# Moving a 128x512 add from VectorE to GpSimd in a message-passing graph kernel

## What is computed

```
h   = relu(layernorm(x))                       # no gain or bias
xn  = layernorm(h) * g1 + b1
msg = relu(xn[src] + edge_attr)
agg = segment_sum(msg, dst)                    # dst is sorted
t   = (1 + eps) * xn + agg
h2  = h + relu(t @ Wg1 + bg1) @ Wg2 + bg2
f   = gelu((layernorm(h2) * g2 + b2) @ Wf1 + bf1) @ Wf2 + bf2
out = x + h2 + f
```

## Time and profile before

| what | value |
|---|---|
| time, median of 3 runs | 1072.53 us (1070.97 to 1072.89) |
| the profiled execution: its own time, its span | 1073.02 us, 1071.3 us |
| TensorE busy | 992.9 us, 93% |
| VectorE busy | 978.7 us, 91% |
| ScalarE busy | 844.3 us, 79% |
| GpSimd busy | 799.9 us, 75% |
| L743, the add that is moved | 33.3 us in 49 instructions |

### The profile page before, as it was taken

How to read it: one execution, slowest core, us unless ns; L and a number is a source line. 1 busy time by engine, 2 the same in 40 slices (tenths; PEclk the granted TensorE clock), 3 DMA queues, 4 the chain that set the end, 5 groups by cost and what they waited for, 6 DMA issues and landing times. The chain is left out here.

```text
span 1071.3 us, 23085 instructions
## 1 busy us (share of the span) xinstructions
PE 992.9 (93%) x6684; PEld 850.1 (79%) x6684; DVE 978.7 (91%) x3499; ACT 844.3 (79%) x2158; POOL 799.9 (75%) x510
## 2 busy tenths in 40 slices
PE   1336999999999999999999999999999999999998
PEld 1225888888888888888888888888888888878887
DVE  5577999999999999999999999999999999988752
ACT  1247888888888888888888888888888888878773
POOL 6488787787787787887887877888878878866610
PEclk9858999999999999999999999999999999999999
DMA  7566676788887655555555554555565654443311
GB/s 234 139 189 161 161 191 185 177 245 233 234 242 216 134 135 130 135 135 127 138 136 123 138 142 118 139 142 117 142 140 114 143 141 112 120 102 92 58 57 40
DMA packets 110469, 156.87 MB, mean 146 GB/s; under 512 B 24836, under 2 KB 50608, under 8 KB 110335
## 3 DMA queue, kind: packets, MB, share of 16 engines
q1 hardware_dynamic: 70358, 128.99, 37.6%
q0 software_dynamic: 37760, 25.66, 19.3%
q10 hardware_dynamic: 2216, 0.66, 0.3%
HBM read 90.61 MB, written 64.61 MB: 145 GB/s over the span
## 5 line engine op out<-in xcount | busy, mean ns | idle before, releaser
L520 ACT ACTIVATE n_act<-p_f,bf1e_col 128x512 f32<-128x512 f32 x392 | 255.9, 679 | 149.4 <-PE p_f L875 141.5
L447 POOL DMA_INDIRECT aggr_sums<-e_merged,e_index x196 | 322.8, 1647 | 65.8 <-issue 49.8
L917 PE MATMUL p_out<-wf,n_act 128*128 128x128 f32 x3136 | 370.6, 276 | 0.0
L917 PEld LDWEIGHTS p_out<-wf,n_act 128*128 128x128 f32 x3136 | 357.6, 191 | 4.0
L456 POOL TENSOR_TENSOR n_rstd<-n_var,minus_half 128x12 f32<-128x12 f32 (+2 forms) x102 | 256.4, 2514 | 116.4 <-DVE n_var L827 59.6
L436 POOL DMA_INDIRECT e_x<-in_x,e_cols x196 | 214.6, 1095 | 61.6 <-issue 58.9
L875 PE MATMUL p_f<-n_z2T_high,wf_low 128*128 128x512 f32 x392 | 207.0, 528 | 11.9 <-issue 7.0
L875 PE MATMUL p_f<-n_z2T_high,wf_high 128*128 128x512 f32 x392 | 154.6, 395 | 0.0
L875 PE MATMUL p_f<-n_z2T_low,wf_high 128*128 128x512 f32 x392 | 153.9, 393 | 0.0
L672 DVE BATCH_NORM_STATS2 n_stat<-n_x 128x6 f32<-128x256 f32 x392 | 139.6, 415 | 0.1
L532 ACT ACTIVATE p_gout<-n_relu,n_rstd 128x128 f32<-128x128 f32 x392 | 129.3, 367 | 5.4 <-DVE n_x L799 5.2
(11 more groups left out here) (85 smaller groups left out, 1433.5 us busy)
## 6 DMA issues: line engine op xcount, KB each, us to landing
n_x<-in_x SPq DMA_DIRECT2D x97, 256.0 KB
n_aggr<-aggr_sums SPq DMA_DIRECT2D x97, 256.0 KB
out_dram<-n_out SPq DMA_DIRECT2D x97, 256.0 KB
aggr_sums<-zeros SPq DMA_DIRECT2D x26, 512.0 KB, 3.2
e_dst<-in_dst_rows SPq DMA_DIRECT2D x49, 256.0 KB
e_attr<-in_attr SPq DMA_DIRECT2D x48, 256.0 KB
aggr_sums<-zeros SPq DMA_DIRECT2D x12, 1024.0 KB
e_x<-in_x,e_cols POOLq DMA_INDIRECT x196
```

What stands on the lines that cost most here:

```text
L447: nc.gpsimd.indirect_dma_start(out=aggr, out_offset=bass.IndirectOffsetOnAxis(ap=e_index[0:r, s, j:j + 1], axis=0), in_=e_merged[0:r, s, j ...
L520: nc.scalar.activation(n_act[:, k, :, 0:b.rows], p_f[k % 2][:, :, 0:b.rows], ACT.Gelu, bias=bf1e_col[:, k:k + 1]).then_inc(s_act, 1)
L917: last = nc.tensor.matmul(p_out[0:b.rows, j, :], n_act[:, k, j, 0:b.rows], wf2[:, k, :], start=False, stop=(k == KF - 1), skip_group_check ...
```

## The change

`add_b1` leaves VectorE. The same instruction, on the same operands and with the same waits, stands in GpSimd's even step behind the first two gathers of a chunk. Its signal `s_eattrb` and the readers of it stay as they are.

```diff
@@ gpsimd, step @@
                 if 0 in halves and (c := edge(0)) is not None:
                     gather(c, range(0, PAIR))
+                if 0 in halves and (c := edge(2)) is not None:
+                    r, s = c.rows, c.slot(3)
+                    if c.is_number(0):
+                        pool.wait_ge(s_rows_out, 1)
+                    pool.wait_ge(q_attr[s], 16 * (c.uses(3) + 1))
+                    reached(pool, s_esum, c.at - 2)
+                    nc.gpsimd.tensor_tensor(e_attrb[0:r, s], e_attr[0:r, s], all_columns(b1_row, r),
+                                            ALU.add).then_inc(s_eattrb, 1)
                 if 1 in halves and 0 in halves:
                     merged_first(edge, apart)
@@ vector @@
-            def add_b1(c):
-
-                if c is not None:
-                    r, s = c.rows, c.slot(3)
-                    if c.is_number(0):
-                        dve.wait_ge(s_rows_out, 1)
-                    dve.wait_ge(q_attr[s], 16 * (c.uses(3) + 1))
-                    reached(dve, s_esum, c.at - 2)
-                    nc.vector.tensor_tensor(e_attrb[0:r, s], e_attr[0:r, s], all_columns(b1_row, r),
-                                            ALU.add).then_inc(s_eattrb, 1)
-
@@ vector, step @@
                 if 0 in halves or not halves:
                     first_half(edge(1), node)
-                    if 0 in halves:
-                        add_b1(edge(2))
```

## The result

| | median of runs | range |
|---|---|---|
| before | 1072.71 us (4 runs) | 1070.97 to 1073.06 |
| after | 1129.88 us (4 runs) | 1129.08 to 1132.31 |

The ratio is 1.0539, 95% interval 1.0522 to 1.0556: the change costs 57 us, 45 us beyond the upper end of the range. The profiled execution took 1129.86 us with a span of 1128.0, which is 56.7 above the span of before.

What follows compares the result with a forecast made beforehand. TensorE and VectorE looked full, VectorE's fullness costing 0.23 us a pair over TensorE's 19.80. 1073.0 - 5.7 (steady) + 1.6 (start) + 1.0 (end) = 1069.9, forecast as 1069.5 us; range 1063 to 1085.

Steps and rivals of the forecast that it cites:

- VectorE's need becomes 20.03 - 0.61 = 19.42 a pair: Steady stretch: without its add, VectorE needs 0.61 us less in each pair, 19.42, below TensorE's 19.80.
- TensorE's 19.80: Steady stretch: TensorE's own pace, 19.80 us a pair, when nobody waits for VectorE.
- VectorE is held up by the add's reads: Rival: VectorE's two-input L840 and L845 stand some 0.9 us while GpSimd's add streams; 1088 us, chance 0.14.
- the add's length: The 128x512 add on GpSimd: 1.25 us, the middle between 0.87 and 1.64.
- the 1.1 worked out beside it: The add on GpSimd by the Trainium skill's 2.6 cycles of 1.2 GHz an element: 1.1 us for 512 elements.
- 19.89: Steady stretch: GpSimd's need in a pair with the add, 20.03 - 1.54 + 1.40, taken as the new pitch.
- gathers land in time: Steady stretch: after the change 2.4 us remain from the last gather's end to VectorE's read; a landing takes 2.42.
- a bound on GpSimd: Rival: two inputs cost twice one, the add takes 1.64 + 0.15, GpSimd becomes the bound; 1086 us, chance 0.13.
- late gathers: Rival: landings take 3.2 us, not 2.42, so VectorE waits 0.8 us in each pair; 1083 us, chance 0.06.
- 1.6 at the start: Before 109 us: adds ahead of later gathers delay VectorE; 1.6 us lost, taken between 0 and 3.2.
- 1.0 at the end: Last chunk: an add stands ahead of its second two gathers; 1.0 us lost, taken between 0 and 1.4.

Runs made afterwards that it cites:

- 1: Changed kernel with GpSimd's add moved ahead of the two gathers, directly behind the second scatter; 1148.9 us, 1.0699 of the kernel before.
- 3: Changed kernel with VectorE's n_out ahead of n_var; 1122.89 us, 1.0438 of the kernel before.
- 6: Changed kernel with the whole add directly behind the odd step's 128x12 `pow`, four e_attr buffers and earlier loads; 1085.96 us, 1.0111 of the kernel before.
- 8: Changed kernel with the whole add behind the odd step's second scatter, one chunk earlier; 1138.26 us, 1.0607 of the kernel before.
- 12: Whole add behind the odd step's `pow`, n_var moved ahead of n_in on VectorE; 1112.12 us, 1.036 of the kernel before.
- 15: Changed kernel with a `pow` of 128x1 between the gathers and the add; 1126.03 us, 1.0498 of the kernel before.
- 5: No add of b1 on any engine, e_attr loaded in the even step into six buffers; 1062.66 us, 0.9892 of the kernel before.
- 13: Whole add behind the odd step's `pow`, n_var between the third and fourth n_in; 1068.38 us, 0.9961 of the kernel before.
- 2: Kernel before, VectorE keeping its add, plus a 128x6 `pow` on GpSimd in the add's place; 1078.47 us, 1.0043 of the kernel before.
- 10: Kernel before, VectorE keeping its add, plus a 128x1408 memset on GpSimd behind the first gathers; 1097.64 us, 1.0227 of the kernel before.
- 16: Whole add behind the odd step's `pow`, n_var between third and fourth n_in, first five chunks added by VectorE; 1064.09 us, 0.9928 of the kernel before.

## Why the prediction was wrong

**The step that failed** is "VectorE's need becomes 20.03 - 0.61 = 19.42 a pair", taken with nothing added. The 19.42 itself holds within 0.25: a single pair less its hold leaves 19.2 to 19.5 (1, 3, 6, 8, 12, 15 and the changed kernel). TensorE's 19.80 holds too (19.82 in 5). But 1.66 us of hold came on top, and by 1, 3, 6, 8, 12 and 13 this depends on what stands beside the add: the same instruction on the same engine costs between 0.1 and 2.3 us a pair, and the pitch follows 19.42 plus the hold, while a longer `pow` in the same place costs no hold (2).

**The rival had the mechanism and not the size.** "VectorE is held up by the add's reads" was given 0.14, a stall of 0.9 and 1088 us. Two things were wrong. The first is the place: it let the add run for 0.4 us before L840 came, since only instructions with two SBUF inputs were counted. Between stands n_var, 128x4, which can be held as well, and which VectorE reaches right behind n_in. The second is the time: the hold began 0.4 us ahead of the add's record, at the end of n_in (502.43 against 502.84), and a gather alone does that to a `tensor_scalar`, as the trace of the kernel before shows (last section). With 1.66 the rival's own formula gives 20.03 - 0.61 + 1.66 = 21.08, and 41 x 1.05 = 43 us for the stretch, where 44.3 were measured.

**What misled the chance** was the row against it, a `pow` that ran beside four L845 without holding them. That was read rightly, and 2 shows it again, but a `pow` of 6 to 16 columns is no model for a stream of 512. The Trainium skill, "SBUF — State Buffer", section "Who interferes with whom", was cited for two SBUF inputs only. The same section also names `tensor_scalar` among the instructions that can contend without a second input, where its operands allow a mode that takes both ports, and says that a GpSimd instruction which only writes leaves two-input instructions alone. The runs agree with both: n_var stood beside the memset and four e_zg did not (10); that n_var is in such a mode no run shows. The section says further that one SBUF input outside such a mode doesn't contend, and the statistics agree (13). By the section a GpSimd instruction that starts first keeps the ports for its whole length, and there the runs differ: a `pow` holds nothing for its length of 1.48 (2).

**What was right:** the add's length (1.25 forecast, the middle of two bounds, taken for want of a reason, so the hit is partly luck; 1.31 measured, 1.26 behind a `pow`, and the 1.1 worked out beside it is too low); that GpSimd isn't the bound (it has 1.5 us a pair to wait in the changed kernel, and with the add in its list it keeps a pitch of 19.81 in 13, so its need is no more than that and not 19.89); that gathers land in time (two short waits in the even stretch of 5, four in that of the changed kernel, 2.1 us together). The rivals of a bound on GpSimd and of late gathers fall.

**The ends.** Forecast were 1.6 at the start and 1.0 at the end; measured 9.25 and 3.2. With a `pow` of such length the start cost 1.7 (2), so the length is rightly priced, and 7.5 are something else. The three kernels with the whole add behind the first gathers start the even stretch at 117.0 to 118.5 us (3, 15, the changed one), all others at 107.4 to 113.5. That ties it to the place; by which chain of waits the 7.5 us come about there was not taken apart, and stays open.

## What to carry to other kernels

Before a streaming instruction goes to GpSimd, look at what VectorE does in that very microsecond. In these runs VectorE's instructions of two SBUF inputs stood until the add ended, small `tensor_scalar`s until an add, a memset or a gather ended, and statistics of one input ran on; so the same add cost 57 us behind the gathers and won 8 beside the statistics (16 against before, with what the buffers bring included). A stall of this kind has no bracket and no row in the waits: look for a short instruction whose mean has grown, and compare its single rows.

## What the runs showed that was not expected

A gather holds a `tensor_scalar` too, with no add near it. In the kernel before:

```profile
482.30 0.43 DVE L810 TENSOR_SCALAR n_minus<-n_stat 128x4 f32<-128x4 f32 x1
...
481.72 1.04 POOL L436 DMA_INDIRECT e_x<-in_x,e_cols  x1 [0.31 <-issue]
```

n_minus, 0.15 long elsewhere, begins 0.58 into the gather and stands until 482.73, the gather's end being 482.76. In 15 n_var does the same (503.31 to 503.74, gather to 503.77), half a microsecond before the add begins. So of the 1.66 on n_var in the changed kernel, the first 0.4 are the gather's.

That is not all of it. In the even stretch of the kernel before no gather lengthens an n_in, yet in four chunks of the changed kernel n_in, of two inputs, is held behind a gather for 1.6 to 1.7 (the burst at 290.22 takes 2.78 for 1.13). Behind a scatter the hold is 2.1 to 2.3, and the add's record begins inside the scatter's and lengthens from 1.26 to 1.85. Behind a `pow` it is about the add's length (1.34 in 15, 1.39 in 12). That part of GpSimd begins the add while the rest is still at the DMA instruction would explain it; it was only argued, no run shows it.

Two smaller things:

- A `pow` of a single column takes 0.59 us (15), where 0.3 was expected from longer ones.
- GpSimd is held too: the 128x12 `pow` takes 2.70 and not 2.31 where it starts beside n_zg and p_out of VectorE (6).
